# Two graph-convolution passes: spans folded on VectorE before the sums by node, and seven of sixteen groups of edges read on TensorE instead of three of eight

## What is computed

```python
def _L1_gnn_ref(edge_index, embedding_weight):
    ...
    norm = deg_inv_sqrt[row] * deg_inv_sqrt[col]
    msgs = embedding_weight[row] * norm[:, None]
    out = jax.ops.segment_sum(msgs, col, num_segments=n)
    return out

def _L2_gnn_ref(features, src, dst, weight, bias):
    ...
    h = features * norm_src[:, None]
    msgs = h[src]
    agg = jax.ops.segment_sum(msgs, dst, num_segments=n)
    agg = agg * norm_dst[:, None]
    out = agg @ weight + bias
    return jax.nn.relu(out)
...
edge_index = jnp.stack([src, dst])
x = _layernorm(x + _L0_gnn_ref(x, edge_index, ...), axis=-1)
x = _layernorm(x + _L1_gnn_ref(edge_index, x), axis=-1)
x = _layernorm(x + _L2_gnn_ref(x, src, dst, ...), axis=-1)
x = _layernorm(x + _L3_gnn_ref(x, edge_index, ...), axis=-1)
```

## Time and profile before

| what | value |
|---|---|
| median of 3 runs | 6187.04 us (6186.88 to 6187.75) |
| profiled execution, its own time | 6186.6 us |
| its span | 6184.8 us |
| PE busy | 5109.1 us, 83% |
| DVE busy | 3377.8 us, 55% |
| POOL busy | 4085.9 us, 66% |
| ACT busy | 1927.7 us, 31% |
| mean granted TensorE clock | 0.928 of full speed |
| pass 1, from its first gather to its closing reduce | 1329.71 to 1989.05 us |
| pass 2, likewise | 2020.85 to 2679.08 us |

### The profile page before, as it was taken

How to read it: one execution, slowest core, us unless ns; L and a number is a source line. 1 busy time by engine, 2 the same in 40 slices (tenths; PEclk the granted TensorE clock), 3 DMA queues, 4 the chain that set the end, 5 groups by cost and what they waited for, 6 DMA issues and landing times.

```text
span 6184.8 us, 144483 instructions
## 1 busy us (share of the span) xinstructions
PE 5109.1 (83%) x50092; PEld 3469.5 (56%) x50092; DVE 3377.8 (55%) x6339; ACT 1927.7 (31%) x3919; POOL 4085.9 (66%) x4227
## 2 busy tenths in 40 slices
PE   1788888868887788758999997699999868999997
PEld 1566666657776677744555555355555534555554
DVE  8223232356566655545666566456666555566656
ACT  0343333335554000013333332333333223333331
POOL 0777777747776777747777771677777437777770
PEclk9899999979998899979999999899999989999998
DMA  1444444423332333324444442344444324444441
GB/s 35 109 112 115 111 116 111 116 76 80 80 80 63 91 80 80 80 53 108 125 124 126 124 125 65 88 124 125 124 126 125 102 61 114 121 126 124 126 122 56
DMA packets 663126, 626.37 MB, mean 101 GB/s; under 512 B 386211, under 2 KB 468170, under 8 KB 662538
## 3 DMA queue, kind: packets, MB, share of 16 engines
q1 hardware_dynamic: 518810, 442.27, 23.6%
q0 software_dynamic: 135360, 174.89, 14.6%
q10 hardware_dynamic: 8368, 1.67, 0.2%
HBM read 529.80 MB, written 88.55 MB: 100 GB/s over the span
## 4 chain that ended last, share of the span: by engine, by line
PE 56%; POOL 17%; issue 15%; DVE 8%; ACT 1%; DVEq 1%; DMA 1%; POOLq 0%
POOL rows L364 17%; PE ps L979 17%; PE ps L823 11%; PE ps L918 8%; PE ps L939 4%; PE ps L838 4%; PE ps L953 3%; PE ps L929 2%; PE ps L898 2%; DVE region L1475 1%; PE ps L850 1%; DVE region L1605 1%; ACT region L615 1%; DVE acc L1438 1%; DMA rows<-table,idx 0%
## 5 line engine op out<-in xcount | busy, mean ns | idle before, releaser
L364 POOL DMA_INDIRECT rows<-table,idx x3172 | 3091.1, 974 | 1461.0 <-issue 1045.2
L979 PE MATMUL ps<-region,hot 128*128 128x272 f32 x4992 | 1325.4, 410 | 116.7 <-DVE region L1583 85.6
L615 ACT ACTIVATE region<-ps 128x512 f32<-128x512 f32 x1248 | 677.4, 594 | 1701.2 <-PE ps L918 1701.2
L979 PEld LDWEIGHTS ps<-region,hot 128*128 128x128 f32 x4992 | 919.2, 194 | 437.5 <-issue 238.0
L1615 DVE TENSOR_TENSOR acc<-acc,ps 128x272 f32 x1248 | 544.1, 436 | 868.7 <-PE ps L979 752.5
L1605 DVE TENSOR_TENSOR region<-ps,region 128x1056 f32<-128x1056 f32 x624 | 779.9, 1251 | 48.3 <-issue 44.9
L823 PE MATMUL ps<-hot,region 128*128 128x192 bf16 (+1 forms) x7488 | 770.2, 265 | 13.2 <-issue 9.6
L823 PEld LDWEIGHTS ps<-hot,region 128*128 128x128 bf16 x7488 | 699.1, 104 | 41.1 <-issue 9.9
L918 PE MATMUL ps<-xT,wcat 64*128 64x512 f32 x2496 | 713.2, 648 | 9.2 <-ACT region L615 9.2
L376 POOL DMA_INDIRECT rows<-table,idx x528 | 501.5, 950 | 259.1 <-issue 160.3
L376 POOL DMA_INDIRECT region<-table,idx x512 | 487.7, 953 | 156.1 <-issue 156.1
(11 more groups left out here) (290 smaller groups left out, 6256.9 us busy)
## 6 DMA issues: line engine op xcount, KB each, us to landing
hot<-hot_dram SPq DMA_DIRECT2D x624, 256.0 KB
turned<-turned_dram SPq DMA_DIRECT2D x624, 128.0 KB
rows<-table,idx POOLq DMA_INDIRECT x3700
hot_dram<-hot SPq DMA_DIRECT2D x104, 512.0 KB
xwin<-table SPq DMA_DIRECT2D x1664, 24.0 KB
region<-hot_dram SPq DMA_DIRECT2D x78, 512.0 KB
turned_dram<-turned SPq DMA_DIRECT2D x104, 256.0 KB
region<-r_dram SPq DMA_DIRECT2D x78, 256.0 KB
```

The source lines that it names most:

```text
L364: pool.indirect_dma_start(rows[:, b, j, :], None, table, bass.IndirectOffsetOnAxis(ap=idx[:, s:s + 1], axis=0)).then_inc(gathered[b], 16)
L615: act.activation(rz[g % 2][:, 2 * t + side, :], ps[:, Z + side, :], ACT.Relu).then_inc(rz_made, 1)
L979: mm = pe.matmul(ps[:, AG + i, 0:PC + H], hot[:, b, 4 * side + 2 * i + j, :], px[b][:, 4 * side + 2 * i + j, :], start=(j == 0), stop=(j = ...
```

## The change

Three things change.

- After each pick DVE folds the 7 spans to one, by a reduce of 448 columns to 64 into the new buffer `found32`. It waits for its own pick and signals `found_made`. PE's dense sum waits for that and has 32 columns instead of 224, and so has the add. `acc` then needs 96 columns a window, not 224: the memset and the closing reduce cover 2400 columns instead of 5600.
- Dense are the groups with 7g mod 16 >= 9, 45 of 104 in place of 39; plain groups are 59 in place of 65. A pass so has 180 dense steps for 156, and 472 gathers for 520.
- `ITEMS` spreads the plain groups evenly: three dense steps, then a plain group, and now and then four.

```diff
-DENSE = [g for g in range(G) if g % 8 in (1, 4, 6)]
-PLAIN = [g for g in range(G) if g % 8 not in (1, 4, 6)]
+DENSE = [g for g in range(G) if 7 * g % 16 >= 9]
+PLAIN = [g for g in range(G) if 7 * g % 16 < 9]
 ND, NP, NS = len(DENSE), len(PLAIN), 4 * len(DENSE)
-AFTER = (1, 4, 6, 9, 11)
-ITEMS = [x for i in range(NS) for x in [("dense", i)] + ([("plain", 5 * (i // 12) + AFTER.index(i % 12))] if i % 12 in AFTER else [])]
+ITEMS = [x for i in range(NS) for x in [("dense", i)] + [("plain", p) for p in range(NP * i // NS, NP * (i + 1) // NS)]]
...
+        found32 = o2[:, 5632:5632 + 512].rearrange("p (b j c) -> p b j c", b=2, j=8)
...
-                pe.wait_ge(picked_made, 4 * dbase + i + 1)
+                pe.wait_ge(found_made, 4 * dbase + i + 1)
...
-                    mm = pe.matmul(ps[:, DB[i % 2], 0:GROUPS * C], dhot[b][:, at, :],
-                                   picked[b][:, at, :, :].rearrange("p g c -> p (g c)"), start=(j == 0), stop=(j == 1))
+                    mm = pe.matmul(ps[:, DB[i % 2], 0:C], dhot[b][:, at, :], found32[:, b, at, :], start=(j == 0),
+                                   stop=(j == 1))
...
-                link(v.memset(acc[:, :, 0:GROUPS * C], 0.0))
+                link(v.memset(acc[:, :, 0:3 * C], 0.0))
...
                                     ).then_inc(picked_made, 1)
+                    v.wait_ge(picked_made, 4 * dbase + i + 1)
+                    if d >= 2:
+                        v.wait_ge(dense_summed, 4 * (d - 1))
+                    v.tensor_reduce(found32[:, d % 2, at:at + 2, :], picked[d % 2][:, at:at + 2, :, :].rearrange(
+                        "p j g c -> p j c g"), AX.X, ALU.add).then_inc(found_made, 1)
...
-                    add(windows["dense"][i % 4], GROUPS * C, ps[:, DB[i % 2], 0:GROUPS * C], dense_added, 4 * dbase + i + 1)
+                    add(windows["dense"][i % 4], C, ps[:, DB[i % 2], 0:C], dense_added, 4 * dbase + i + 1)
...
-                link(v.tensor_reduce(summed, acc[:, :, 0:GROUPS * C].rearrange("p w (k c) -> p w c k", k=GROUPS), AX.X, ALU.add))
+                link(v.tensor_reduce(summed, acc[:, :, 0:3 * C].rearrange("p w (k c) -> p w c k", k=3), AX.X, ALU.add))
```

More of the change, by code:

```diff
@@ L294, in build @@
         bt_made, dense_read, picked_made = sem("bt_made"), sem("dense_read"), sem("picked_made")
+        found_made = sem("found_made")
         dense_summed, dense_added = sem("dense_summed"), sem("dense_added")
```

## The result

The changed kernel takes 6095.9 us (median of 4 runs, 6080.6 to 6103.9), the kernel before on the same chip 6187.0 us: a ratio of 0.9849 with a 95% interval of 0.9836 to 0.9861. So 91 us are gained where the prediction had 116. The profiled execution of the changed kernel took 6103.9 us, with a span of 6102.2.

The account below looks back on a forecast made before the run. POOL's gathers were taken to bound both convolution passes. Gains of 50.3 us in pass 1, 55.3 in pass 2 and 2 x 5.4 in the closing reduces make 116 us: 6071 us forecast, range 6050 to 6122.

Parts of the forecast that it names:

- POOL, 60.3 us less a pass: Gathers on POOL: 48 fewer a pass at 1.257 us each, so 598.9 us a pass if POOL stays the bound.
- The fold at 0.93 us, the first bullet's extrapolation: DVE's new reduce of 448 columns, priced at 0.93 us from two rows in groups of seven: 1.68 ns a column, 0.17 fixed.
- The rival of 1.10 us: DVE's fold costs 1.10 us, twice the row of half its size: 6118 us in all, chance 0.21.
- Add of 32 columns and PE's sum: In a dense step, DVE's add takes 0.14 us after overlap, and PE's sum of four passes 0.46 us.
- Closing reduce: DVE's reduce ending each pass, 2400 columns for 5600: 4.2 us for 9.57, 5.4 less a pass.
- The other price, by outputs: Closing reduce priced by its 800 outputs, unchanged in number: some 6.2 us, 3.4 less a pass.
- How DVE and PE meet, pass 1: DVE waits for PE's reads 0.25 us a period, 15 in all, on 594.5 bare: pass 1 takes 609 us.
- the walk: One period of a plain and three dense steps followed on PE and DVE: DVE waits about 0.25 us.
- Pass 2: Second convolution pass: DVE 585 us, under POOL's 599, plus 4 for reads at the low clock: 603, 55 less.
- POOL as the bound of both passes: Rival: the fold costs less than 0.85 us or DVE's waits vanish, so gathers set both passes: 6056 us, chance 0.29.
- The slower rival: PE loses its clock every period, one read a plain group 2.0 us longer, no gather hiding it: 6287 us, chance 0.07.
- The markers given ahead: Right if DVE is busy over 90% of pass 1, clock 0.93 or more; wrong if DVE waits over 0.5 us a period.

Follow-up runs that it names:

- e1: The kernel before with the new lists (45 dense, 59 plain groups, even order), without the fold: 6068.6 us, ratio 0.9823.
- short fold: The changed kernel with a reduce over three of seven spans, part of the sums left out, on two other chips: ratios 1.0086 and 1.0087.
- e3: The changed kernel with eight idle matmuls in the second dense step behind each plain group, ahead of PE's wait: 6065.5 us, ratio 0.9805.
- e0: The changed kernel run again, unaltered, beside the kernel before: 6094.4 us, ratio 0.9857.
- f2: The changed kernel with its reduce over three of seven spans, repeated on another chip: 8232.3 us against 8160.9 for the kernel before.

## Why the prediction came out as it did

The sign and the range are right, the size is 25 us short. Step by step, on the first chips:

- **POOL, 60.3 us less a pass.** Right where POOL is the bound: e1 has both passes at 601.8 against the 598.9 worked out; the 3 us between are in the pitch, 1.264 us (1335.93 to 1931.16 over 471 steps) where 1.257 was taken.
- **The fold at 0.93 us, the first bullet's extrapolation.** Right: 926 ns. The rival of 1.10 us falls.
- **Add of 32 columns and PE's sum.** Right or a little better: the add takes 0.18 us, PE's four matmuls 0.39 apart (1439.02 to 1439.41) against 0.46.
- **Closing reduce.** Mis-sized: 2.86 instead of 4.2 us, 6.7 less each instead of 5.4. The term took 1.68 ns a column from groups of seven; in groups of three a column costs (2861 - 170) / 2400 = 1.12 ns, and in the short fold (373 - 170) / 192 = 1.06. The other price, by outputs, falls too.
- **How DVE and PE meet, pass 1.** Mis-sized: DVE waited 49 us for reads where the walk had 15, and the pass is 38 us longer (646.8 for 609). The walk started both engines of a period together and had PE reach its next sum as the fold ends. But PE is ahead of DVE: in the period of the slow read above it begins its plain sum 1.64 us before DVE's one-hot.

```profile
1446.01 0.51 PE L851 MATMUL ps<-rows,region 128*128 128x96 bf16 x8
...
1447.65 1.20 DVE L1481 TENSOR_TENSOR region<-dloc,ps 128x1024 bf16<-128x1024 f32 x1
```

So it stands there for the fold. That alone costs nothing, since DVE is the later one. But the prediction said "After the change PE idles less per wait, by the walk well below a microsecond, so I expect the granted clock in the passes to rise, not to fall": this is the step that failed. PE did idle less per wait, 1.6 us on average where it was 2.4, but not below a microsecond, and the granted clock in pass 1 went from 0.91 to 0.92 only. The slow reads stayed as many as before, 26 for 25, with 39 us in them, and the sum had nothing for them in pass 1, where the gathers had hidden them until then. e3 shows what they cost: with shorter waits the reads hold 3 us above 2.22, and the pass is 36 us shorter than in e0, 609.8.
- **Pass 2.** Right in size: 607.8, 602.2 and 605.3 against 603. Fewer reads are slow (11, 8 and 9), and POOL's gathers cover most of what they cost; the allowance of 4 us was for them.
- **The rivals.** POOL as the bound of both passes needed the waits to vanish; they did not, and with the fold pass 1 was never below 609.8. The slower rival named the true mechanism, a slow read behind a wait with no gather to hide it, but priced it at every period, with a chance of 0.07; what happened lies between: 26 slow reads for 59 periods, at 1.4 us each, not 2.0. It should have stood in the sum of the forecast as a part, not only outside it.

The markers given ahead: the clock rose only from 0.91 to 0.92 in pass 1 and from 0.90 to 0.95 in pass 2, DVE was busy for 82% of pass 1 (530.8 of 646.9), not 90%, and waited 0.84 us a period, over the 0.5 named as a sign of error. Late gathers in pass 1, behind a wait for the plain sum, came as forecast: 15, for 21 us in all.

Sum in the profiled executions: 12.5 and 50.4 us in the passes, 13.4 in the closing reduces, 76 of the 83 between 6186.6 and 6103.9. The other 6 lie in stages that the change doesn't touch: the first gather comes 5.3 us later than before (1335.03 for 1329.71), and what follows the second closing reduce is 11.5 us shorter. No run says why, and by e0, e1 and e3 these stages differ from one execution to the next by as much.

The best kernels of the study are e3 and e1, 6065.5 and 6068.6 us, not to be told apart; both beat the kernel before and the change. e1 is the simpler, and has neither fold nor filler.

## What to carry to other kernels

Where an engine is given a new instruction between another engine's step and the next, ask not only who is late, but how long the engine that is early stands still, and if it is TensorE, what its next step costs at the low clock and what covers it. Count also the losses that a busier engine hides before the change: ask which of these waits the change removes, which it adds, and what still covers them. Take each part of a change alone before keeping both: here the split brought 119 us, the fold 17, and both 93. And a kernel balanced to within 1% between two engines on one chip can be out of balance on another: what a move of work to TensorE gained here was lost where TensorE stood idle in the middle of its reads.

## What the hardware showed that I had not expected

- Waits of PE of 1.0 to 2.2 us were followed by a read at the low clock in 26 of 57 cases in pass 1 and 11 of 57 in pass 2; the length alone doesn't decide it (over 1.8 us it was 8 of 12 in pass 1, 8 of 17 in pass 2). The Trainium skill, TensorE: Matmul & The Clock Gate, A second HAM failure mode: psum-queue depth-cycling, describes TensorE idling briefly but often between groups of matmuls, with the clock going back and forth; the trace agrees, with 26 slow reads behind such waits in pass 1.
- Eight matmuls that compute nothing, 0.8 us a time, ahead of PE's longer waits gave back 29 us of 6094 (e3).
- A column of a strided reduce on DVE cost 1.68 ns in groups of seven and 1.06 to 1.12 in groups of three, both at a stride of 32 float32 columns, less 0.17 us a time (an estimate from the two rows of seven).
- On two chips the same program took 32 to 35% longer, with TensorE standing idle in the middle of its reads (293.9 us ahead of L824 in f2, under what the view calls issue), while POOL, ACT and DVE were busy for about as long as on the first chip.
